# Moving the own-edge additions of the second graph convolution into the middle of the layer norm, on one Trainium2 core

## The chip, the core and the metric

The kernel runs on one core of a Trainium2 chip. Five engines work side by side and meet only at semaphores: TensorE (PE, with its weight loads PEld), VectorE (DVE), ScalarE (ACT), GpSimd (POOL) and SyncE (SP), which issues the DMA transfers here. The metric is the device time of one execution in microseconds. Before the change it is 3359.72 us, the median of three runs (3355.37 to 3362.7).

## The reference

Four graph layers are applied one after the other to `x`, 3125 nodes of 128 features, over 53125 edges with self loops, each as `x = x + layer(relu(layernorm(x)))`. The change touches the first half of the second layer, a graph convolution followed by a layer norm and a SiLU:

```python
def _gcn_conv(x, src, dst, W, b, num_nodes):
    h = x @ W
    deg = jnp.zeros((num_nodes,), h.dtype).at[dst].add(1.0)
    dinv = jnp.where(deg > 0, jax.lax.rsqrt(jnp.maximum(deg, 1.0)), 0.0)
    norm = dinv[src] * dinv[dst]
    msg = h[src] * norm[:, None]
    out = jnp.zeros((num_nodes, h.shape[1]), h.dtype).at[dst].add(msg)
    return out + b
...
h = _gcn_conv(h, src, dst, gcn_w, gcn_b, num_nodes)
h = _silu(_layernorm(h, ln_gamma, ln_beta))
h = _gat_conv(h, src, dst, gat_w, att_src, att_dst, gat_b, num_nodes, HEADS)
```

The sum over edges is computed as a product with the adjacency matrix (counts of edges, in float16), to which each node's edge to itself is added.

## The kernel before, in words

`gcn_second` (from L1148) does the second convolution. The 3125 target nodes are cut into eight chunks of 1, 3, 3, 3, 3, 4, 4 and 4 tiles of 128 nodes (`GCN_TILES`), here chunk 0 to chunk 7. For one chunk the five engines do this:

- SP (L1172) loads the chunk's columns of the adjacency matrix into one of two buffers of `cols` (`gcn_adj` in the trace). Chunk c + 2 goes into the buffer of chunk c and is issued when all five casts of chunk c are done.
- DVE adds the own edges (`add_own`, L1223): one small addition of an identity per tile into `cols`. It waits for the load. Its last addition raises `own_in`.
- POOL casts the chunk to fp32r for the matmul (`widen`, L1210), in five groups of five source tiles each, into a ring of four slots `stream` (`gcn_stream`). The first cast of a chunk waits for `own_in`; cast n waits until PE has streamed group n - 4.
- PE does two matmuls for each of 25 source tiles t (L1306). Between them it turns the sums of the chunk before to node order (`turn`, L1281, at t = 5) and, at t = 22, turns that chunk's finished values back to feature order (`turn_back`, L1290), for which it waits for the SiLU of that chunk.
- ACT copies the sums out of PSUM (L1197), takes the square root (L1180), the SiLU (L1182) and the copy of the result (L1188).
- DVE does `norm(c)`: scale and bias from PSUM (L1232), `bn_stats` (L1237), `bn_aggr` (L1241), the addition of epsilon (L1244), then it waits for the square root (`rooted`), reciprocal (L1246), shift (L1248), one scaling per tile (L1251), times gamma (L1254), plus beta (L1256). Each step waits for the one before by the semaphore `steps`.

So norm(c) runs while PE streams chunk c + 1, and its end is what `turn_back` in that same stream waits for. The order on every engine is written out by hand; there is no scheduler. The loop that sets DVE's order is L1268 to L1271.

Of the kernel before, what the change touches and what calls it, by code (L numbers as in the profile page):

```python
# [77 lines left out]
NGC = 8  # L78
# [119 lines left out]
def over_nodes(ap, nt=NT):  # L198

    return ap.unsqueeze(1).to_broadcast([ap.shape[0], nt, ap.shape[1]])  # L200
# [261 lines left out]
class Kernel:  # L462
# [687 lines left out]
    def gcn_second(self, own, parts, out, ht, rows, weights, cols, stream, loaded):  # L1150
# [15 lines left out]
        with nc.Block() as block:  # L1166
            @block.sync
            def _(e):
                for c, (lo, hi) in enumerate(spans):
                    if c >= 2:  # L1170
                        e.wait_ge(widened, NGG * (c - 1))
                        e.dma_start(cols[:, c % 2, 0:(hi - lo) // W, :], self.adj[:, lo // W:hi // W, :]).then_inc(loaded[c % 2], 16)  # L1172
# [43 lines left out]
            @block.vector  # L1216
            def _(e):
                def add_own(c):

                    e.wait_ge(loaded[c % 2], 16 * (c // 2) + 16)  # L1220
                    for i, (t, p) in enumerate(tiles[c]):
                        at = cols[:, c % 2, 8 * i:8 * i + p // W, t * W:(t + 1) * W]
                        inst = e.tensor_tensor(at, at, ident_h[:, 0:p].rearrange("p (w n) -> p w n", n=W), ALU.add)  # L1223
                    inst.then_inc(own_in, 1)

                def norm(c):

                    t0, t1 = tiles[c][0][0], tiles[c][-1][0] + 1
                    at, two = slice(t0, t1), range(t0, t1)
                    e.wait_ge(turned, c + 1)  # L1230
                    for q, (t, p) in enumerate(tiles[c]):
                        inst = e.scalar_tensor_tensor(out[0:p, t, :], ps[0:p, 2 + c % 2, q * P:(q + 1) * P], self.dinv[0:p, t:t + 1],  # L1232
                                                      bias[0:p, :], ALU.mult, ALU.add)
                    inst.then_inc(steps, 1)
                    e.wait_ge(steps, per * c + 1)
                    for t in two:
                        inst = e.bn_stats(out=stats[:, t, :], in_=out[:, t, :])  # L1237
                    inst.then_inc(steps, 1)
                    e.wait_ge(steps, per * c + 2)
                    for t in two:  # L1240
                        inst = e.bn_aggr(out=both[:, t, :], in_=stats[:, t, :])  # L1241
                    inst.then_inc(steps, 1)
                    e.wait_ge(steps, per * c + 3)
                    e.tensor_scalar(scale[:, at], both[:, at, 1], EPS, None, ALU.add).then_inc(steps, 1)  # L1244
                    e.wait_ge(rooted, c + 1)
                    e.reciprocal(scale[:, at], scale[:, at]).then_inc(steps, 1)  # L1246
                    e.wait_ge(steps, per * c + 5)
                    e.scalar_tensor_tensor(shift[:, at], both[:, at, 0], -1.0, scale[:, at], ALU.mult, ALU.mult).then_inc(steps, 1)  # L1248
                    e.wait_ge(steps, per * c + 6)
                    for t in two:  # L1250
                        inst = e.tensor_scalar(out[:, t, :], out[:, t, :], scale[:, t:t + 1], shift[:, t:t + 1], ALU.mult, ALU.add)  # L1251
                    inst.then_inc(steps, 1)
                    e.wait_ge(steps, per * c + 7)
                    e.tensor_tensor(out[:, at, :], out[:, at, :], over_nodes(gamma[:], t1 - t0), ALU.mult).then_inc(steps, 1)  # L1254
                    e.wait_ge(steps, per * c + 8)
                    e.tensor_tensor(out[:, at, :], out[:, at, :], over_nodes(beta[:], t1 - t0), ALU.add).then_inc(steps, 1)  # L1256

                e.tensor_copy(ident_h[:], self.ident[:])
                e.memset(out[:, NT - 1, :], 0.0).then_inc(begun, 1)
                e.wait_ge(begun, 1)  # L1260
                add_own(0)
                for n in range(NT // grp):
                    at = slice(n * grp, (n + 1) * grp)
                    e.wait_ge(near, n + 1)
                    e.tensor_tensor(parts[:, at, 1, :], own[:, at, :], parts[:, at, 0, :], ALU.subtract).then_inc(far, 1)
                add_own(1)
                weights(e, begun)
                for c in range(NGC):  # L1268
                    if c + 1 >= 2 and c + 1 < NGC:
                        add_own(c + 1)  # L1270
                    norm(c)  # L1271

            @block.tensor
# [1730 lines left out]
```

## Time and profile before

| | |
|---|---|
| median of three runs | 3359.72 us |
| profiled execution | 3363.56 us, span 3361.9 us |
| busy: PE, DVE, ACT, POOL | 83%, 52%, 41%, 29% of the span |
| second convolution | about 417 to 525 us of the span |
| casts L1210, all 40 | 417.6 to 509.8 us |

The profile is of one execution, with times counted from the span's start. The second convolution is about 3% of the span. A row of a timeline merges neighbouring instructions of one line: start, length of the whole group, engine, line, operation, written and read tensors, and `xN` for the count; what stands in brackets is the idle time before it and what ended it. Idle time of an engine counts only where another engine then waits.

### The profile page before, as it was taken

What the parts mean: (1) busy time and instruction counts of PE and PEld (TensorE: products, weight loads), DVE (VectorE), ACT (ScalarE), POOL (GpSimd) and SP (SyncE); (2) the same over time, 40 slices, a digit from 0 to 9 for tenths busy, and PEclk for the clock granted to TensorE, in tenths of its full rate; (3) what the DMA queues carried; (4) which work ended last, traced back from release to release, by engine and by line L of the source; (5) the groups of instructions that cost most, each with busy time, mean ns of one, the idle gap of its engine ahead of it and who ended that gap; (6) DMA issues with size and microseconds to landing.
All of it is one profiled execution on the core that took longest, in us unless ns stands there. A gap on an engine that the chain in (4) does not pass through costs nothing. (4 is left out here: it accounts for less than half of the span.)

```text
span 3361.9 us, 41194 instructions
## 1 busy us (share of the span) xinstructions
PE 2803.2 (83%) x13998; PEld 2153.0 (64%) x13998; DVE 1752.6 (52%) x4008; ACT 1368.4 (41%) x2596; POOL 965.7 (29%) x786
## 2 busy tenths in 40 slices
PE   6778797999996999999999999999744455447997
PEld 3446684777774778778887877786433344435775
DVE  8997657999977351121111112112544443356994
ACT  4573134999996121111111111111413333342896
POOL 6110070000000643223222322220177777740000
PEclk9998897999998999999999999999855555555999
DMA  4434352111002432212121212210242221113200
GB/s 151 144 105 157 137 200 88 40 40 77 8 1 92 162 117 88 79 59 98 59 94 68 88 64 98 85 64 5 87 129 47 46 55 29 29 19 128 79 35 20
DMA packets 79695, 266.66 MB, mean 79 GB/s; under 512 B 21129, under 2 KB 53344, under 8 KB 70176
## 3 DMA queue, kind: packets, MB, share of 16 engines
q1 hardware_dynamic: 62520, 236.50, 18.9%
q0 software_dynamic: 16976, 27.54, 3.8%
q8 instruction: 121, 1.98, 0.3%
q14 instruction: 78, 0.64, 0.1%
HBM read 232.80 MB, written 31.18 MB: 79 GB/s over the span
## 5 line engine op out<-in xcount | busy, mean ns | idle before, releaser
L2798 PE MATMUL psum<-gate_stream,parts 128*128 128x384 f32 (+1 forms) x3600 | 668.8, 344 | 15.9 <-POOL gate_stream L2871 11.6
L2798 PEld LDWEIGHTS psum<-gate_stream,parts 128*128 128x128 f32 x3600 | 632.4, 189 | 32.9 <-issue 13.4
L2871 POOL CAST gate_stream<-gate_adj 128x1920 fp32r<-128x1920 f16 (+1 forms) x200 | 370.6, 1860 | 851.9 <-PE psum L2798 829.7
L2150 PE MATMUL psum<-gat_h,gat_pair 128*128 128x129 f32 (+1 forms) x3750 | 571.9, 292 | 8.6 <-DVE gat_pair L1954 7.8
L2150 PEld LDWEIGHTS psum<-gat_h,gat_pair 128*128 128x128 f32 (+1 forms) x3750 | 462.4, 191 | 123.3 <-issue 77.9
L1482 POOL DMA_INDIRECT edge_rows<-edge_table,src_idx x440 | 429.8, 977 | 181.4 <-issue 133.8
L2889 DVE SCALAR_TENSOR_TENSOR gate_work<-psum,bhh,gate_work 128x384 f32<-128x384 f32 (+1 forms) x80 | 50.0, 626 | 793.7 <-PE psum L2761 763.1
L1954 DVE SCALAR_TENSOR_TENSOR gat_pair<-gat_above,gat_adj 128x512 f32<-128x512 f32 (+3 forms) x525 | 326.4, 622 | 87.7 <-PE psum L2150 58.7
L2063 ACT ACTIVATE gat_above<-psum,gat_as 128x512 f32<-128x512 f32 (+3 forms) x525 | 329.4, 627 | 42.7 <-PE psum L2138 41.0
L2054 ACT ACTIVATE psum<-gat_ad_rows,gat_as 128x512 f32<-128x512 f32 (+3 forms) x525 | 334.9, 638 | 16.8
L1909 DVE SCALAR_TENSOR_TENSOR gat_acc<-gat_adj,gat_q,gat_acc 128x512 f32<-128x512 f16 (+3 forms) x497 | 328.3, 677 | 0.0
L2815 ACT COPY x<-psum 128x384 f32<-128x384 f32 (+1 forms) x72 | 31.8, 488 | 545.5 <-PE psum L2798 545.5
L1719 PE MATMUL psum<-edge_rows,edge_hot 128*128 128x81 f32 x826 | 179.6, 418 | 85.7 <-DVE edge_rows L1618 85.7
L1719 PEld LDWEIGHTS psum<-edge_rows,edge_hot 128*128 128x128 f32 x826 | 177.2, 332 | 87.4 <-issue 87.0
L966 PE MATMUL psum<-count_hot,count_low 128*128 128x400 f16 x611 | 171.2, 382 | 50.6 <-DVE count_hot L887 34.5
L2138 PE MATMUL psum<-gat_r_rows,gat_pick 6*128 6x512 bf16 (+7 forms) x525 | 189.4, 362 | 0.9 <-ACT gat_r_rows L2072 0.9
L2843 ACT ACTIVATE gate_work<-psum,brz 128x384 f32<-128x384 f32 (+1 forms) x80 | 47.0, 587 | 331.7 <-PE psum L2774 331.7
L966 PEld LDWEIGHTS psum<-count_hot,count_low 128*128 128x128 f16 x611 | 87.4, 144 | 136.2 <-issue 112.7
L887 DVE TENSOR_SCALAR count_hot<-iota_hot,keyt 128x400 f16<-128x400 f16 x611 | 168.6, 336 | 3.0 <-PE psum L966 2.4
L2382 POOL MEMSET parts<- 128x512 f32 x1 | 0.5, 524 | 546.2 <-POOLq L2282 546.2
L981 ACT CAST count_stage<-psum 128x400 f16<-128x400 f32 x196 | 96.7, 493 | 91.6 <-PE psum L966 89.4
L1646 ACT ACTIVATE edge_hot<-iota,edge_minus 128x128 f32<-128x128 f32 x413 | 121.3, 392 | 8.0 <-PEq L2457 8.0
(484 smaller groups left out, 3700.1 us busy)
## 6 DMA issues: line engine op xcount, KB each, us to landing
gate_adj<-adj SPq DMA_DIRECT2D x35, 2400.0 KB, 8.1
gat_adj<-adj SPq DMA_DIRECT2D x8, 3200.0 KB, 10.8
adj<-count_stage SPq DMA_DIRECT2D x196, 100.0 KB, 1.7
gcn_adj<-adj SPq DMA_DIRECT2D x8, 2400.0 KB, 8.1
edge_place<-row_scratch SPq DMA_DIRECT2D x40, 352.0 KB, 3.6
gate_adj<-adj SPq DMA_DIRECT2D x5, 2800.0 KB, 9.0
gcn_adj<-adj SPq DMA_DIRECT2D x4, 3200.0 KB, 10.0
edge_rows<-edge_table,src_idx POOLq DMA_INDIRECT x440
```

Of the source, the lines that this page charges most:

```text
L887: e.tensor_scalar(hot[:, j % HRING, :], iota_hot[:], keyt[:, j:j + 1], None, ALU.is_equal).then_inc(hots, 1)
L966: e.matmul(flat[:, bass.ds(at[j % RL], ROW)], low[:, j // LS % LRING, :, j % LS], hot[:, j % HRING, :], start=False, stop=False, skip_grou ...
L1482: e.indirect_dma_start(out=rows[:, c % 2, s, 0:ROWS], out_offset=None, in_=table, in_offset=bass.IndirectOffsetOnAxis(ap=self.src_idx[:, k ...
L1719: mm = e.matmul(flat[:, bass.ds(to[k % 4], SUMS)], hot_of(c)[:, s, :], rows[:, c % 2, s, :], start=False, stop=False, skip_group_check=True)
L1909: e.scalar_tensor_tensor(on, of, q[:, hi, h:h + 1], on, ALU.min, ALU.max).then_inc(most, 1)
L1954: e.scalar_tensor_tensor(on(pair, g % 2), on(above, g % 3), 1e30, cols[:, u % ring, 0:width(u) // W, hi * W:(hi + 1) * W], ALU.min, ALU.mu ...
L2054: e.activation(ps[:, 4 + g % 3, 0:up - lo], ad_rows[:, h, lo:up], ACT.Relu, bias=as8[:, hi, h:h + 1], scale=1.0 - NEG).then_inc(relus, 1)
L2063: e.activation(above[:, g % 3, 0:width(u)], ps[:, 4 + g % 3, 0:width(u)], ACT.Exp, bias=as2[:, hi, h:h + 1]).then_inc(exps, 1)
L2138: e.matmul(ps[:, 4 + g % 3, 0:width(u)], pick[:, h, :], r2_rows[:, u % 2, 0:width(u)], start=False, stop=False, skip_group_check=True).the ...
L2150: mm = e.matmul(ps[0:p, b, a:a + D + 1], pair[:, g % 2, i * P:i * P + p], h1[:, hi, h, :], start=hi == 0 and i % 3 == 0, stop=hi == NT - 1 ...
L2798: mm = e.matmul(ps[:, f, 0:hi - lo], parts[:, t, m, f, :], stream[:, (NGG * i + t // GG) % GR, 0:windows(i), t % GG * W:(t % GG + 1) * W], ...
L2871: e.tensor_copy(stream[:, n % GR, 0:windows(i), :], cols[:, i % 2, 0:windows(i), g * GW:(g + 1) * GW]).then_inc(widened, 1)
```

## The change

The own edges of chunk c + 2 are no longer added after norm(c) but inside it: behind the addition of epsilon and ahead of the wait for the square root. Chunks 2 to 7 are concerned; chunks 0 and 1 keep their place ahead of the loop. The two new lines shift the later line numbers by two: L1246, L1248, L1251, L1254 and L1256 become L1248, L1250, L1253, L1256 and L1258.

```diff
@@ -1242,6 +1242,8 @@
                     inst.then_inc(steps, 1)
                     e.wait_ge(steps, per * c + 3)
                     e.tensor_scalar(scale[:, at], both[:, at, 1], EPS, None, ALU.add).then_inc(steps, 1)
+                    if c + 2 < NGC:
+                        add_own(c + 2)
                     e.wait_ge(rooted, c + 1)
                     e.reciprocal(scale[:, at], scale[:, at]).then_inc(steps, 1)
                     e.wait_ge(steps, per * c + 5)
@@ -1266,8 +1268,6 @@
                 add_own(1)
                 weights(e, begun)
                 for c in range(NGC):
-                    if c + 1 >= 2 and c + 1 < NGC:
-                        add_own(c + 1)
                     norm(c)
```

DVE's instructions from the epsilon of chunk 1 to the own edges of chunk 3, before (`h_23` is the convolution's output, `gcn_ident` the identity):

```order
L1244 TENSOR_SCALAR gcn_scale<-gcn_both 128x3
L1246 RECIPROCAL gcn_scale<-gcn_scale 128x3
L1248 SCALAR_TENSOR_TENSOR gcn_shift<-gcn_both,gcn_scale 128x3
L1251 TENSOR_SCALAR h_23<-h_23,gcn_scale,gcn_shift 128x128 x3
L1254 TENSOR_TENSOR h_23<-h_23,ln_gamma 128x384
L1256 TENSOR_TENSOR h_23<-h_23,ln_beta 128x384
L1223 TENSOR_TENSOR gcn_adj<-gcn_adj,gcn_ident 128x8x16 x3
```

The same stretch of DVE after the change:

```order
L1244 TENSOR_SCALAR gcn_scale<-gcn_both 128x3
L1223 TENSOR_TENSOR gcn_adj<-gcn_adj,gcn_ident 128x8x16 x3
L1248 RECIPROCAL gcn_scale<-gcn_scale 128x3
L1250 SCALAR_TENSOR_TENSOR gcn_shift<-gcn_both,gcn_scale 128x3
L1253 TENSOR_SCALAR h_23<-h_23,gcn_scale,gcn_shift 128x128 x3
L1256 TENSOR_TENSOR h_23<-h_23,ln_gamma 128x384
L1258 TENSOR_TENSOR h_23<-h_23,ln_beta 128x384
```

The three additions of L1223 have moved past six lines of the norm. The other engines' instructions stand in the same order as before; on POOL the first cast of chunk 3 still waits for the last of these three additions.

## Rows read from the trace of the kernel before

**Rows 1.** Engine busy times by stretch, the stretches from chunk 1's turn to chunk 7's.
```profile
core 0: us, PE busy (x) PEld busy (x) DVE busy (x) ACT busy (x) POOL busy (x), PEclk, DMA share, GB/s
441.88:515.68 73.80, 65.15 (x331) 55.74 (x329) 42.19 (x128) 25.20 (x37) 53.63 (x27) 1.00 0.41 162
```

**Rows 2.** Waits of 417 to 526 us: us in total, times, longest.
```profile
PE psum L1290 <- ACT h L1182: 12.9, 7, 6.7
PE psum L1306 <- POOL gcn_stream L1210: 1.8, 4, 0.9
```

**Rows 3.** Timeline of DVE, second half of the norm of chunk 2.
```profile
454.62 0.76 DVE L1244 TENSOR_SCALAR gcn_scale<-gcn_both 128x3 f32<-128x3 f32 x1
455.65 0.18 DVE L1246 RECIPROCAL gcn_scale<-gcn_scale 128x3 f32<-128x3 f32 x1 [0.27 <-ACT gcn_scale L1180]
455.86 1.25 DVE L1248 SCALAR_TENSOR_TENSOR gcn_shift<-gcn_both,gcn_scale 128x3 f32<-128x3 f32 x1
457.14 0.86 DVE L1251 TENSOR_SCALAR h<-h,gcn_scale,gcn_shift 128x128 f32<-128x128 f32 x3
...
459.11 0.49 DVE L1223 TENSOR_TENSOR gcn_adj<-gcn_adj,gcn_ident 128x128 f16<-128x128 f16 x3
```

**Rows 4.** Timeline of POOL: the casts of chunks 3, 4, 6 and 7.
```profile
448.36 8.73 POOL L1210 CAST gcn_stream<-gcn_adj 128x1920 fp32r<-128x1920 f16 x5 [3.21 <-DVE gcn_adj L1223]
459.66 8.74 POOL L1210 CAST gcn_stream<-gcn_adj 128x1920 fp32r<-128x1920 f16 x5 [2.56 <-DVE gcn_adj L1223]
...
485.19 11.41 POOL L1210 CAST gcn_stream<-gcn_adj 128x2560 fp32r<-128x2560 f16 x5 [2.70 <-DVE gcn_adj L1223]
499.79 10.08 POOL L1210 CAST gcn_stream<-gcn_adj 128x2240 fp32r<-128x2240 f16 x5 [3.19 <-DVE gcn_adj L1223]
```

**Rows 5.** Timeline of PE: the turns back of chunk 0 and chunk 2.
```profile
438.95 0.27 PE L1290 MATMUL psum<-ident,h 128*128 128x128 f32 x1
...
459.80 0.55 PE L1290 MATMUL psum<-ident,h 128*128 128x128 f32 x3 [1.21 <-ACT h L1182]
```

**Rows 6.** Timeline of ACT, chunk 0.
```profile
435.98 0.31 ACT L1182 ACTIVATE h<-h 128x128 f32<-128x128 f32 x1 [0.16 <-DVE h L1256]
```

**Rows 7.** Groups by form: count | busy us, mean ns of one | idle before.
```profile
L1248 DVE SCALAR_TENSOR_TENSOR gcn_shift<-gcn_both,gcn_scale 128x3 f32<-128x3 f32 x4 | 4.4, 1105 | 0.1
L1244 DVE TENSOR_SCALAR gcn_scale<-gcn_both 128x3 f32<-128x3 f32 x4 | 4.1, 1023 | 0.1
L1248 DVE SCALAR_TENSOR_TENSOR gcn_shift<-gcn_both,gcn_scale 128x4 f32<-128x4 f32 x3 | 3.4, 1144 | 0.1
L1244 DVE TENSOR_SCALAR gcn_scale<-gcn_both 128x4 f32<-128x4 f32 x3 | 2.0, 661 | 0.1
```

**Rows 8.** The gated layer, DVE additions beside POOL casts: timelines, and L2904's durations (min/median/max).
```profile
1130.01 9.92 POOL L2871 CAST gate_stream<-gate_adj 128x1920 fp32r<-128x1920 f16 x5 [7.63 <-PE psum L2798]
...
1132.35 4.20 DVE L2904 TENSOR_TENSOR state<-gate_work 128x384 f32<-128x384 f32 x2
...
L2904 DVE TENSOR_TENSOR state<-gate_work x80: 548/550/2414, 1132.4 to 2344.5; 128x384 f32<-128x384 f32 x70, 128x448 f32<-128x448 f32 x10
```

**Rows 9.** A tensor_scalar with a column scalar: durations min/median/max.
```profile
L887 DVE TENSOR_SCALAR count_hot<-iota_hot,keyt x611: 302/314/8215, 35.9 to 292.2; 128x400 f16<-128x400 f16 x153
```

**Rows 10.** Two stretches after a pause of PE, columns as in rows 1.
```profile
1218.00:1221.40 3.40, 3.40 (x14) 3.12 (x13) 1.32 (x2) 0.68 (x2) 0.92 (x1) 0.50 0.00 0
...
2344.40:2351.20 6.80, 5.74 (x7) 2.52 (x8) 1.74 (x6) 0.24 (x1) 0.70 (x3) 0.50 0.17 52
```

**Rows 11.** Timeline of PE around those pauses.
```profile
1216.65 0.63 PE L2734 MATMUL psum<-ident,state 128*128 128x128 f32 x4 [2.88 <-DVE parts L2912]
1217.04 1.06 PE L2798 MATMUL psum<-gate_stream,parts 128*128 128x448 f32 x4
1218.58 1.84 PE L2798 MATMUL psum<-gate_stream,parts 128*128 128x448 f32 x4
...
2345.46 3.75 PE L2491 MATMUL psum<-state,l 128*128 128x512 f32 x4 [4.34 <-PEq L2710]
```

## Prediction

> **What bounds the kernel now.** I read the busy times by stretch first. From the turn of chunk 1 to that of chunk 7, 73.80 us, TensorE is busy for 65.15 us [rows 1]; DVE and POOL have slack. So at most 8.65 us is to be had from PE's gaps here, 0.26% of the whole. The waits then say who holds PE: the SiLU ahead of the turn back, 7 times, 12.9 us, of which 6.7 us is the last one, behind the stream; and the POOL casts, 4 times, 1.8 us [rows 2]. The SiLU waits for DVE's norm. Thus in each chunk from 1 on the norm's length sits on PE's path: turn, norm, SiLU, turn back, 6 + 10 matmuls, next turn.
>
> The timelines of DVE and POOL are to be laid over each other [rows 3, 4]. In the norm of chunk 2 the epsilon addition, three numbers per partition, takes 0.76 us, the shift 1.25 us; the reciprocal between them, of the same size, 0.18 us. The five casts of chunk 3 run from 448.36 to 457.09, one per 1.75 us, so one ends near 455.35 and the last at 457.09. The epsilon ends at 455.38 and the shift at 457.11: each waited for the end of a cast. From 457.14 on POOL is idle, and the rest of the norm (L1251, L1254, L1256) runs free. It is idle because the own edges of chunk 4 come only at 459.11 + 0.49; the next cast starts at 459.66 [rows 3, 4]. POOL's 2.56 us of idle time is what shields the tail of the norm.
>
> That such waits come for every such instruction is seen in the gated layer: two additions of 128x384 with both inputs in SBUF take 4.20 us together beside casts, 2.1 us each, where the median of the line is 0.55 us; and five casts take 9.92 us instead of 8.73 [rows 8, 4]. DVE and POOL take turns, one instruction each, though DVE's next is ready.
>
> The Trainium skill states this as a rule (SBUF — State Buffer, Who interferes with whom): DVE and GpSimd share a port pair under an exclusive lock held for the whole instruction; a DVE instruction with two SBUF inputs contends with a GpSimd one that reads SBUF, and tensor_scalar can too. By that rule, with which these rows agree, the change is a harmful one.
>
> **The change part by part.** Nothing is added or removed in count; 21 additions of own edges, of chunks 2 to 7, move from behind the norm into its middle.
>
> *Own edges.* Three cost 0.49 us, four about 0.62 (0.14 us more for each). 0.27 us of it lies under the wait for the square root [rows 3]: +0.22 or +0.35 us, for norms 0 to 5 three times each, +1.7 us. The reciprocal then lies under the first cast, 0.2 us six times, -1.2. Net +0.5 us.
>
> *Casts in the tail.* When the own edges of chunk c + 2 are in, its first cast starts. Its ring slot is free: it needs the second group of chunk c + 1, which PE finished before norm(c) began its epsilon. The second and third cast need the third and fourth group, which PE streams at 1.8 us each before it stops at t = 22; the fourth cast needs the last group, which lies behind the turn back. So exactly three casts fall into the tail. The tail's instructions that want the shared port are the shift, L1251 once per tile, L1254, L1256: more than three, each followed by a gap for a dependence or a dispatch. By the alternation seen in [rows 8], the three casts stand in the norm in full: shift behind the first, the first L1251 behind the second, the others behind the third. Prices, by start to start in [rows 4]: 1.75 us for 128x1920, 2.28 for 128x2560 (11.41 / 5), 2.02 for chunk 7. Chunks 2 to 4: 9 x 1.75 = 15.7; chunks 5 and 6: 6 x 2.28 = 13.7; chunk 7: 3 x 2.02 = 6.1. Together +35.5 us.
>
> The doubtful part is whether L1251 wants the port. An epsilon addition is a tensor_scalar and does [rows 3]; one with a column scalar, L887, does 400 elements in 0.314 us [rows 9], more than one element per ns, so the form has the fast mode as well. I take it that it does. If not, the L1251s run under the second cast: 0.86 us in norms 1 to 4, about 1.1 in norm 5, 0.35 in norm 0, so 4.9 us less.
>
> The skill's page names tensor_scalar from SBUF to SBUF as able to use both ports; by it the sum keeps these 4.9 us, and no row here shows a two-column form beside a cast.
>
> *Norm 0 has slack.* Its SiLU ends at 435.98 + 0.31 while PE comes to the turn back at 438.95, unheld [rows 5, 6]: 2.6 us of its three casts are hidden. Its own edges meet a last cast of chunk 1, +0.3. Together -2.3 us.
>
> *What goes.* The last cast of chunk c + 1 starts about when turn(c) does and ends before the epsilon, since POOL is now ahead. A free instruction of this size takes near the 0.18 us of the reciprocal [rows 3], say 0.17. Epsilon: 4.1 + 2.0 us for seven, less 7 x 0.17, 4.9 us. Shift: 4.4 + 3.4 less 7 x 0.16 is 6.7 us [rows 7]; the first cast's wait is already among the three. PE's waits for casts: 1.8 us [rows 2]. Together -13.4 us. Norm 6 has no own edges and gains only; PE can use all but 0.3 us of it, +0.3.
>
> Sum so far: 0.5 + 35.5 - 2.3 - 13.4 + 0.3 = +20.6 us.
>
> *TensorE's clock.* PE waits 1.2 us for the SiLU today [rows 5] and would wait some 4.5 to 6 us in chunks 2 to 6, near 3 in chunk 1. The granted clock is 1.00 in this stage [rows 1]. After pauses of 2.88 and 4.34 us it was 0.50, that is 1.2 instead of 2.4 GHz, for stretches of 3.40 and 6.80 us, with PE busy for 3.40 and 5.74 us of them [rows 10, 11]. Four matmuls then took 1.84 us and not 1.06 [rows 11], so 43% of the busy time is lost. Lower end 0 (no fall). Upper end: all 16 matmuls between turn back and turn at half clock, 2.9 us of them becoming 5.1, 6 x 2.2 = 13. I take the shorter of the two stretches, 0.43 x 3.4 = 1.46 us, six times: +8.8 us.
>
> Total +29.4 us: 3363.56 + 29.4 = 3393.0 in a profiled execution. That one ran 3.8 us above the median of the runs, so for the median 3359.7 + 29.4 = 3389.1 us, 0.9% slower.
>
> **Rivals.** A measurement of this kernel tells some 0.2%, 6.7 us, from no change.
>
> *A, part of the price.* L1251 doesn't want the port (15.7 us), or the clock holds (20.6), or it holds and L1251 is out too: 3375 to 3384 us. For it: the two-column form takes 0.29 us a tile, no quicker than an addition would; against: rows 9, and no pause above 2.8 us in these rows without a fall.
>
> *B, one cast only.* If DVE's queued instructions went ahead of the next cast, only the first would be paid: 35.5 becomes 11.8, sum -3.1 without stalls for the clock, 3357 us. Against it stand the two additions of 4.20 us.
>
> *C, faster.* The tail is shielded after all, if the ring slot for the first cast of chunk c + 2 became free only after the norm: POOL's 13.4 us of waits in norm and stream would go and nothing come. PE can give at most its 8.65 us of gaps, less own edges: about -7, 3353 us. It decides at the second group of chunk c + 1: streamed after the norm's end, C; before the epsilon, my case. That group is done some 2 us after turn(c), the epsilon 2.5 us after it.
>
> *D, the load is late.* Own edges now wait 3.7 us earlier for the load of chunk c + 2, with DVE's tail behind them. The load is issued at the last cast of chunk c, which also moves ahead, by 3 us or more. If it were late by 2 us in five norms: +10 more, 3399 us.
>
> **How the numbers follow.** My case (all three casts, L1251 among the held, clock falling) 0.55; A 0.27; D 0.06; B 0.08; C 0.04. The forecast is my case's 3389 us. Low: A's lower half reaches 3375, and B and C lie outside; with part of a cast less than I count, 3368. High: the clock's upper end adds 4, a little of D the rest: 3400. Slower by over 0.2%: my case, A and D, 0.88; within 0.2%: B, 0.08; faster: C, 0.04.
>
> **What would show it.** Right: the casts of chunk c + 2 start right behind L1223 in the middle of norm(c), three in a row, a pause, then two; epsilon near 0.17 us, shift near 1.6 (2.1 beside 128x2560), L1251 three in over 2 us, one of L1254 or L1256 free; norms of 10 to 12 us instead of 5.5 to 8.5; PE waiting some 25 us in total for the SiLU within the stream, none for casts; a clock of 0.50 in stretches between 440 and 540 us. L1251 unmoved at 0.86 us and L1254 and L1256 both long: A. Tail as before: B or C. Waits of L1223 for a load: D. All outside this stage should stay.

## Result: 0.65% slower, and the profile after

| | median | runs | profiled execution | from the first turn to the eighth |
|---|---|---|---|---|
| before | 3359.93 us | 6 | 3363.56 us | 432.83 to 515.68, 82.85 us |
| after | 3380.12 us | 6 | 3375.06 us | 432.74 to 539.41, 106.67 us |

The ratio is 1.0065, 95% interval 1.0054 to 1.0075; on 3359.7 us that is 18 to 25 us. The forecast was 3389 us, range 3368 to 3400. The measure for the stage in all that follows is the time from the start of the turn of chunk 0 to the start of that of chunk 7 (L1281 on PE); it grew by 23.8 us. The two profiled executions differ by 11.5 us only, because the one after was the fastest of its six, and lies 5 us below their median, and the one before 4 us above its own. The stage is where the change is to be read, the medians say what it costs.

The timeline of DVE after the change, in the norms of chunk 0 and chunk 2 (start, length, engine, line, operation, count):

```profile
435.07 0.15 DVE L1248 RECIPROCAL gcn_scale<-gcn_scale 128x1 f32<-128x1 f32 x1
435.25 1.76 DVE L1250 SCALAR_TENSOR_TENSOR gcn_shift<-gcn_both,gcn_scale 128x1 f32<-128x1 f32 x1
437.04 1.77 DVE L1253 TENSOR_SCALAR h<-h,gcn_scale,gcn_shift 128x128 f32<-128x128 f32 x1
438.85 1.76 DVE L1256 TENSOR_TENSOR h<-h,ln_gamma 128x128 f32<-128x128 f32 x1
440.64 0.29 DVE L1258 TENSOR_TENSOR h<-h,ln_beta 128x128 f32<-128x128 f32 x1
...
460.98 0.87 DVE L1232 SCALAR_TENSOR_TENSOR h<-psum,dinv,gcn_bias 128x128 f32<-128x128 f32 x3 [6.77 <-PE psum L1281]
...
462.94 0.17 DVE L1244 TENSOR_SCALAR gcn_scale<-gcn_both 128x3 f32<-128x3 f32 x1
463.02 0.49 DVE L1223 TENSOR_TENSOR gcn_adj<-gcn_adj,gcn_ident 128x128 f16<-128x128 f16 x3
...
463.63 1.74 DVE L1250 SCALAR_TENSOR_TENSOR gcn_shift<-gcn_both,gcn_scale 128x3 f32<-128x3 f32 x1
465.41 3.75 DVE L1253 TENSOR_SCALAR h<-h,gcn_scale,gcn_shift 128x128 f32<-128x128 f32 x3
469.20 0.56 DVE L1256 TENSOR_TENSOR h<-h,ln_gamma 128x384 f32<-128x384 f32 x1
469.79 0.56 DVE L1258 TENSOR_TENSOR h<-h,ln_beta 128x384 f32<-128x384 f32 x1
```

The same stretch of POOL, the casts of chunk 2 and of chunk 4:

```profile
435.21 5.26 POOL L1210 CAST gcn_stream<-gcn_adj 128x1920 fp32r<-128x1920 f16 x3 [0.41 <-DVE gcn_adj L1223]
442.78 3.54 POOL L1210 CAST gcn_stream<-gcn_adj 128x1920 fp32r<-128x1920 f16 x2 [2.31 <-PE psum L1306]
...
463.58 5.25 POOL L1210 CAST gcn_stream<-gcn_adj 128x1920 fp32r<-128x1920 f16 x3 [1.10 <-DVE gcn_adj L1223]
473.85 3.65 POOL L1210 CAST gcn_stream<-gcn_adj 128x1920 fp32r<-128x1920 f16 x2 [5.02 <-PE psum L1306]
```

In norm 2 the epsilon is free now (0.17 us against 0.76 in [rows 3]) and the own edges follow it. Then three casts run from 463.58 to 468.83; DVE's shift, first and second scaling each stand behind one of them, and the rest of the norm's tail (times gamma and plus beta, L1256 and L1258) is free from 469.20 on. The norm, L1232 to L1258, takes 9.37 us (460.98 to 470.35) and not 6.54. Norm 0 shows the turn-taking at its plainest: three different instructions of 0.15 to 0.35 us in rows of 1.76, 1.77, 1.76, one per 1.80 us. Three casts, a pause until PE has turned back, two casts: as the ring of four slots allows.

The waits of the stretch 417 to 546 us (total, times, longest), the answer to [rows 2]:

```profile
POOL gcn_stream L1210 <- PE psum L1306: 32.8, 10, 6.5
...
PE psum L1290 <- ACT h L1182: 24.1, 6, 5.8
```

PE waits 24.1 us for the SiLU inside the stream, where it waited 6.2; it waits for no cast any more. And the clock, busy times by stretch with the columns of [rows 1], and PE's timeline at the turns back of chunks 0 and 1:

```profile
432.74:539.41 106.67, 81.94 (x384) 73.27 (x382) 64.01 (x140) 28.79 (x42) 61.48 (x31) 0.87 0.34 135
441.33:444.31 2.98, 2.98 (x18) 2.94 (x19) 0.00 (x0) 1.81 (x3) 1.53 (x1) 1.00 0.23 97
453.40:460.20 6.80, 5.38 (x18) 5.38 (x19) 0.77 (x2) 2.76 (x4) 1.79 (x1) 0.50 0.01 2
```

```profile
441.33 0.33 PE L1290 MATMUL psum<-ident,h 128*128 128x128 f32 x1 [2.28 <-ACT h L1182]
441.41 3.06 PE L1306 MATMUL psum<-gcn_stream,gcn_parts 128*128 128x384 f32 x16
...
454.82 0.90 PE L1290 MATMUL psum<-ident,h 128*128 128x128 f32 x3 [4.06 <-ACT h L1182]
455.37 5.24 PE L1306 MATMUL psum<-gcn_stream,gcn_parts 128*128 128x384 f32 x16
```

After a wait of 2.28 us the clock stays at 1.00 and 16 matmuls take 3.06 us; after one of 4.06 us it is 0.50 (1.2 GHz) from 453.4 to 460.2 and they take 5.24.

### The profile page after: what moved, and what is told of

The parts are those of the page before. It is cut to its first block and busy times, and to the rows that moved or that the text cites. A ratio compares the mean times of both kernels' runs of the same rounds, so it can differ in the third digit from the quotient of the medians.

```text
span 3373.4 us, 41194 instructions
## 1 busy us (share of the span) xinstructions
PE 2794.7 (83%) x13998; PEld 2147.6 (64%) x13998; DVE 1771.9 (53%) x4008; ACT 1368.4 (41%) x2596; POOL 965.2 (29%) x786
## 3 DMA queue, kind: packets, MB, share of 16 engines
q8 instruction: 121, 1.98, 0.2%
## 5 line engine op out<-in xcount | busy, mean ns | idle before, releaser
L2798 PE MATMUL psum<-gate_stream,parts 128*128 128x384 f32 (+1 forms) x3600 | 667.1, 344 | 15.9 <-POOL gate_stream L2871 11.5
L2798 PEld LDWEIGHTS psum<-gate_stream,parts 128*128 128x128 f32 x3600 | 630.8, 188 | 32.7 <-issue 13.4
L1482 POOL DMA_INDIRECT edge_rows<-edge_table,src_idx x440 | 429.3, 976 | 178.9 <-issue 133.8
L1210 POOL CAST gcn_stream<-gcn_adj 128x1920 fp32r<-128x1920 f16 (+3 forms) x40 | 74.5, 1890 | 182.8 <-DVE gcn_adj L1223 150.0
```

The lines of the kernel that those rows point to most:

```text
L1482: e.indirect_dma_start(out=rows[:, c % 2, s, 0:ROWS], out_offset=None, in_=table, in_offset=bass.IndirectOffsetOnAxis(ap=self.src_idx[:, k ...
L2798: mm = e.matmul(ps[:, f, 0:hi - lo], parts[:, t, m, f, :], stream[:, (NGG * i + t // GG) % GR, 0:windows(i), t % GG * W:(t % GG + 1) * W], ...
```

## The experiments

Each edit is to the kernel after, if nothing else is said. "Stage" is the time between the same two turns, from the profile of that kernel; the "tail" of a norm is its part behind the own edges, from the shift on. Ratios are to the kernel before, run beside it on the same chip.

| | stage, us | median, us | ratio (95%) |
|---|---|---|---|
| before | 82.85 | | 1 |
| after | 106.67 | 3380.12 | 1.0065 (1.0054 to 1.0075) |
| after again (e8) | 106.89 | 3380.25 | 1.0066 (1.0053 to 1.0080) |
| casts held until the norm is over (e1) | 84.44 | 3362.78 | 1.0010 (1.0001 to 1.0019) |
| one cast let into the norm (e2) | 83.53 | 3360.29 | 1.0003 (0.9994 to 1.0012) |
| PE kept busy in its pauses (e3) | 99.39 | 3379.12 | 1.0056 (1.0043 to 1.0068) |
| the same, longer in chunk 4 (e7) | 97.87 | 3374.21 | 1.0045 (1.0031 to 1.0058) |
| scalings on ACT (e5) | 103.31 | 3722.04 | 1.0057 (1.0043 to 1.0070) |
| after again, other chip (e6) | 109.49 | 3728.78 | 1.0063 (1.0042 to 1.0084) |
| kernel before, one cast in five on ACT (e4) | 75.72 | 3352.90 | 0.9982 (0.9973 to 0.9992) |

**e1, the casts held, the own edges still in the middle.**

```diff
                     if g == 0:
                         e.wait_ge(own_in, c + 1)
+                        if c >= 2:
+                            e.wait_ge(steps, per * (c - 1))
```

> The changed kernel, but POOL's first cast of chunk c + 2 also waits until the norm of chunk c is over; the own edges stay in the middle of the norm. Theory (casts stand between the instructions of the norm's tail at the shared port, and PE's longer pauses bring its clock down): norms of 5.7 to 8.7 us as before plus 0.2 to 0.35 us, turn 0 to turn 7 near 83 us instead of 106.7, clock 1.00 throughout, 3357 to 3362 us. Rival (the moved additions themselves, or the load that they now wait for earlier, lengthen the norm): norms stay at 9 to 11 us and the time near 3380 us.

Measured: ratio 1.0010, stage 84.44 us, 1.6 above before and 22.2 below after. What costs is what the move lets start, and not the move itself. The rival is out. Three expectations missed: the norms of chunks 2 to 5 grew by 0.6 to 0.8 us and not by 0.2 to 0.35; the clock was 0.98 in the mean of the stage, with one short fall; and the median of 3362.78 us is just above 3362. The norm of chunk 2 shows why the norms grew by more:

```profile
455.94 0.76 DVE L1246 TENSOR_SCALAR gcn_scale<-gcn_both 128x3 f32<-128x3 f32 x1
456.60 2.15 DVE L1225 TENSOR_TENSOR gcn_adj<-gcn_adj,gcn_ident 128x128 f16<-128x128 f16 x3
458.68 0.16 DVE L1250 RECIPROCAL gcn_scale<-gcn_scale 128x3 f32<-128x3 f32 x1
```

With the casts back at their old time, the last one of chunk 3 falls between the own edges: 2.15 us instead of 0.49, of which the shift's old wait is gone (0.16 instead of 1.25 us in [rows 3]). The fall of the clock comes behind the turn back of chunk 5:

```profile
502.65 1.10 PE L1292 MATMUL psum<-ident,h 128*128 128x128 f32 x4 [1.98 <-ACT h L1182]
```

The 1.6 us of the stage are a sum of three terms, read from the times of turns and turns back in the two profiles. The stretches from a turn to its turn back, in which the norms lie, are 1.9 us longer in all; those from the turns back of chunks 1 to 4 to the next turn are 1.7 us shorter; and the one behind the turn back of chunk 5, with the low clock, is 1.3 us longer (5.51 instead of 4.19 us).

**e2, one cast inside.**

```diff
                     if g == 0:
                         e.wait_ge(own_in, c + 1)
+                    if g == 1 and c >= 2:
+                        e.wait_ge(steps, per * (c - 1))
```

> The changed kernel, but only the first cast of chunk c + 2 may start inside the norm of chunk c; the second waits for the norm's end. Theory (each cast in the tail is paid once, less the fixed part of the instruction that it holds): shift 1.75 to 2.3 us as in the changed kernel, the scalings free at 0.86 us, norms of 6.4 to 8.2 us, no wait for the epsilon, 3357 to 3363 us. Rival (POOL's early start as such, by any number of casts, costs the whole 20 us): 3375 us or more.

Measured: 1.0003, no change, and the stage 0.7 us above before. In the norm of chunk 3:

```profile
467.28 0.77 DVE L1246 TENSOR_SCALAR gcn_scale<-gcn_both 128x3 f32<-128x3 f32 x1
467.95 0.62 DVE L1225 TENSOR_TENSOR gcn_adj<-gcn_adj,gcn_ident 128x128 f16<-128x128 f16 x4
468.49 0.17 DVE L1250 RECIPROCAL gcn_scale<-gcn_scale 128x3 f32<-128x3 f32 x1
468.69 2.28 DVE L1252 SCALAR_TENSOR_TENSOR gcn_shift<-gcn_both,gcn_scale 128x3 f32<-128x3 f32 x1
471.01 0.86 DVE L1255 TENSOR_SCALAR h<-h,gcn_scale,gcn_shift 128x128 f32<-128x128 f32 x3
```

One cast in, one instruction held: the shift 2.28 us beside a cast of 128x2560, the scalings 0.86 us again. "No wait for the epsilon" was wrong: four casts still come after the norm and reach into the next one. One cast in each tail costs the stage next to nothing, three cost it 24 us: the price goes with the number of casts in the tail, not with POOL's early start.

**e5, which instruction is held does not matter.** The scaling per tile (L1253) is taken from DVE; ACT does it as an activation with scale and bias.

```diff
+                    e.wait_ge(steps, per * c + 6)
+                    for t in range(t0, t1):
+                        inst = e.activation(out[:, t, :], out[:, t, :], ACT.Identity, scale=scale[:, t:t + 1], bias=shift[:, t:t + 1])
+                    inst.then_inc(steps, 1)
...
-                    for t in two:
-                        inst = e.tensor_scalar(out[:, t, :], out[:, t, :], scale[:, t:t + 1], shift[:, t:t + 1], ALU.mult, ALU.add)
-                    inst.then_inc(steps, 1)
```

> The changed kernel, with the scalings (L1253, one per tile) done by ACT, so that only the shift and the two long additions of the tail want the port. Theory (DVE and POOL take turns whatever the instructions are, and three casts are ready in each tail): still three casts in the tail, one ahead of the shift, one ahead of the product with gamma, one ahead of the addition of beta; norms of 8.6 to 9.0 us for 3 tiles beside casts of 128x1920, 0.4 to 0.8 us less than in the changed kernel, since the scaling runs under the second cast; 3374 to 3378 us. Rival (the two-column scaling is what the casts collide with): norms of 6.5 to 7 us and 3362 us or less.

Measured on another chip, on which the whole kernel takes 3703 us before and 3729 after; the durations on DVE and POOL are the same there, so the ratio and the stage are read, not the microseconds expected. The norms of 3 tiles beside casts of 128x1920 took 8.59 us (466.71 to 475.30 for chunk 1), as expected, and three casts stood in each tail. DVE's and POOL's timelines in the norm of chunk 1:

```profile
469.37 1.75 DVE L1254 SCALAR_TENSOR_TENSOR gcn_shift<-gcn_both,gcn_scale 128x3 f32<-128x3 f32 x1
472.52 0.73 DVE L1257 TENSOR_TENSOR h<-h,ln_gamma 128x384 f32<-128x384 f32 x1 [1.41 <-ACT h L1183]
473.28 2.02 DVE L1259 TENSOR_TENSOR h<-h,ln_beta 128x384 f32<-128x384 f32 x1
```

```profile
469.31 5.59 POOL L1214 CAST gcn_stream<-gcn_adj 128x1920 fp32r<-128x1920 f16 x3 [1.10 <-DVE gcn_adj L1227]
```

The third cast now stands ahead of the addition of beta, which takes 2.02 us instead of 0.56; the second runs mostly beside ACT's scalings and holds the product with gamma for the rest, 0.73 us. The rival is out: the scaling was only what happened to be next. Beside the changed kernel on the same chip (e6) the stage is 6.2 us shorter, of which 4.3 us lie between turn and turn back; the ratios, 1.0057 and 1.0063, do not tell the two apart.

**e3 and e7, the clock.** Ahead of the wait for the SiLU PE does small matmuls of constants into an unused bank; e7 has 48 of them in chunk 4.

```diff
                         if c and t == 22:
+                            if c < NGC - 1:
+                                self.keep_busy(e, ps[:, 6, :], 20 if c == 1 else 34)
                             turn_back(c - 1)
```

> The changed kernel, with 34 small matmuls (20 in chunk 1) of constants into an unused PSUM bank ahead of each wait for the SiLU in chunks 1 to 6, some 3.6 us of work for PE in its pause. Theory (part of the loss is the clock that falls after the pauses): clock 1.00 from 433 to 540 us, 16 matmuls of 128x384 between turn back and turn in 3.1 us instead of 4.1 to 5.2, 6 to 9 us faster than the changed kernel, 3371 to 3374 us, norms unchanged. Rival (the clock costs nothing, since what it slows is hidden): 3378 to 3382 us.

Measured: the stage 7.3 us shorter, with one fall of the clock left, behind the longest pause (chunk 4). The total, 1.0056, was above the expected 3371 to 3374 us, and its interval overlaps that of the kernel after; it could not tell the theory from the rival. So a version with the longest pause closed as well (e7) and the changed kernel (e8) were run side by side.

> e3_busy with 48 instead of 34 small matmuls in chunk 4, whose pause is the longest (5.8 us), beside the unchanged changed kernel on the same chip. Theory (the clock costs some 7 us of the changed kernel): clock 1.00 in the whole stage, turn 0 to turn 7 near 98 us, and a time 5 to 10 us below that of e8_again, the ratio to the kernel before near 1.004. Rival (what the clock gives in the stage is lost elsewhere, as the totals of e3_busy left open): the same ratio as e8_again within 2 us.

> The changed kernel, the partner of e7_busy2. Theory: ratio to the kernel before 1.006 to 1.007, turn 0 to turn 7 of 105 to 110 us, depending on where the clock falls after each pause. Rival: a ratio near 1.004 or below would say that the first comparison was high by chance.

Measured: 3374.21 against 3380.25 us, 6.0 us, and in the stage 97.87 against 106.89 us, 9.0 us. The intervals of the two ratios overlap a little, but each of the five runs of e7 (3369.82 to 3376.93 us) lies below each of the five of e8 (3378.38 to 3382.47). In e7 the whole stretch, and the 16 matmuls after the turn back of chunk 2, read:

```profile
432.50:531.00 98.50, 96.22 (x591) 85.27 (x591) 63.97 (x140) 29.13 (x42) 61.44 (x31) 1.00 0.37 146
```

```profile
468.62 0.55 PE L1290 MATMUL psum<-ident,h 128*128 128x128 f32 x3 [0.33 <-ACT h L1182]
468.92 3.05 PE L1308 MATMUL psum<-gcn_stream,gcn_parts 128*128 128x384 f32 x16
```

The clock is 1.00 throughout. DVE's 63.97 us busy are those of the kernel after, 64.01: nothing changed in the norms. So 9.0 us of the stage's 24 are the clock. The other 15 remain at full clock: what the casts cost at the port, less what became free. Whether all of the 9.0 reach the total stays open; 6.0 were seen, and in the profiles 1.6 us of the 9.0 are lost again just behind the stage (54.4 us from the last turn to the first of the matmuls with `gat_pair` in e7, 52.9 in e8).

**e6, the changed kernel a second time.**

> The changed kernel once more, for a second profile. Theory: turn 0 to turn 7 again within 2 us of 106.7 us, whatever the whole takes, and 3375 to 3385 us; differences of more than 3 us between two profiles lie outside the second convolution. Rival (the whole and the stage vary together): the stage differs by as much as the whole does.

Measured: 1.0063 on the chip of 3703 us. The stage was 109.49 us, 2.8 above the first, where 2 were expected. All eight norms had the lengths of the first profile within 0.06 us. Of the 2.8 us, 2.5 lie between turns back and turns, where PE waits for nothing and its clock sets the time. One difference is that the clock also fell behind the turn back of chunk 0, after a wait as short as 2.32 us, and it took 4.2 us from there to the next turn instead of 3.0:

```profile
461.02 0.33 PE L1290 MATMUL psum<-ident,h 128*128 128x128 f32 x1 [2.32 <-ACT h L1182]
462.00:465.50 3.50, 3.50 (x15) 3.41 (x14) 0.00 (x0) 1.76 (x2) 1.82 (x2) 0.57 0.00 0
```

So what varies in the stage is the clock; and e8, on a chip like the first, gave 106.89.

**e4, a version that beats both.** If casts, tail and own edges queue at one port, the remedy is less work there. In the kernel before, ACT does the first cast of chunks 2 to 7 behind the SiLU, with a semaphore of its own (`acted`) for PE and for the load; POOL does the other four.

```diff
                     e.activation(out[:, t0:t1, :], out[:, t0:t1, :], ACT.Silu).then_inc(eased, 1)
+                    if c + 2 < NGC:
+                        n, k = NGG * (c + 2), (spans[c + 2][1] - spans[c + 2][0]) // W
+                        e.wait_ge(own_in, c + 3)
+                        e.wait_ge(streamed, n - GS + 1)
+                        e.copy(stream[:, n % GS, 0:k, :], cols[:, c % 2, 0:k, 0:GW]).then_inc(acted, 1)
...
-                    for g in range(NGG):
+                    for g in range(1 if c >= 2 else 0, NGG):
                         widen(c, g)
```

> The kernel before, with the first of the five casts of chunks 2 to 7 done by ACT behind the SiLU, four left to POOL. Theory (the five casts, the norm's tail and the own edges follow one another at the shared port and make the period of a chunk of 11.3 us, above PE's 10.3): casts end 1.75 to 2.3 us earlier, epsilon and shift wait less, PE's waits for the SiLU nearly go, 4 to 8 us faster than before, 3352 to 3356 us. Rival (ACT's cast delays its copy of the sums and the square root, and PE waits there): 3359 us or slower.

Measured: 0.9982 (0.9973 to 0.9992), stage 75.72 us, 7.1 less than before. Beside it, DVE in the norm of chunk 2 and POOL's and ACT's casts:

```profile
455.00 0.78 DVE L1253 TENSOR_SCALAR gcn_scale<-gcn_both 128x3 f32<-128x3 f32 x1
...
456.25 0.17 DVE L1257 SCALAR_TENSOR_TENSOR gcn_shift<-gcn_both,gcn_scale 128x3 f32<-128x3 f32 x1
```

```profile
458.97 7.00 POOL L1219 CAST gcn_stream<-gcn_adj 128x1920 fp32r<-128x1920 f16 x4 [3.22 <-DVE gcn_adj L1232]
```

```profile
458.96 1.79 ACT L1191 CAST gcn_stream<-gcn_adj 128x1920 fp32r<-128x1920 f16 x1
```

The shift no longer waits, and a norm takes 5.47 us (453.03 to 458.50) instead of 6.54. ACT's cast takes 1.79 us while POOL's beside it keep their 1.75 each, so the two do not hold each other up. PE's wait for the SiLU within the stream is down to 0.3 us in total, and from the turn of chunk 2 to that of chunk 3 it is 10.23 us (452.50 to 462.73) instead of 11.32 (452.12 to 463.44). So the chain of five casts, the shift held by the last of them, the tail and the own edges set the chunk's period before as well. How much of the 7.1 us is the port and how much POOL's shorter queue was not told apart.

## Why the prediction was right, point by point

- *Where the time goes* was right in its main steps: own edges early, first cast right behind, three casts in the tail, a pause, two more; epsilon free; L1253 among the held; norm 0 partly covered; no wait for a load. e1, e2 and e5 show it from three sides. Of the signs that I named, two missed: the norms took 9.4 us (chunks 1 and 2) to 11.3, not 10 to 12, and both L1256 and L1258 were free, not one of them.
- *The price of the casts* was the mis-sized term. I counted each cast with its full 1.75, 2.28 or 2.02 us and then the held instruction's own time as well. Most of that time runs under the cast. Norm 0 shows it: slots of 1.79 to 1.81 us that hold an instruction which free takes 0.16, 0.35 and 0.29 us; so a cast adds 1.60, 1.42 and 1.47 us. In norms 1 and 2 the shift adds 1.75 - 0.16 and the scalings 3.75 - 0.86 us, together 4.5 where I had 5.2; in norms 3 and 4 it is (2.28 - 0.16) + (4.82 - 0.86) = 6.1 against 6.8; norm 5 (2.02 - 0.16) + (4.54 - 1.12) = 5.3 against 6.1. Over six norms 4.5 + 9.0 + 12.2 + 5.3 = 31 us and not 35.5. With it the sum without the clock is 16.1 us; the stage of e7, whose clock does not fall, is 15.0 above before. The profiles show where the last 1 us is. The stretches from turn to turn back are 17.9 us longer in e7 than before (74.19 against 56.26), which is the mended sum without PE's waits for casts. The stretches from turn back to turn are 2.9 us shorter (23.68 against 26.59), where I had put 1.8 for those waits. Why it is more was not followed.
- *The clock* was put at 8.8 us by six stalls of 1.46; measured 9.0 in the stage, by five. From the turn back to the next turn the kernel after takes 5.63, 4.52, 5.22, 5.39 and 6.32 us and e7 3.21, 3.19, 3.78, 4.12 and 3.95: a fall cost 1.3 to 2.4 us, 1.8 in the mean, and not most behind the longest wait. The wait of 2.28 us in chunk 1 brought no fall, those of 3.8 to 5.8 us all did. That 8.8 came so near to 9.0 is luck: six falls too cheap against five dearer ones.
- *What goes* (13.4 us) was right in kind: epsilon and shift of norm 6 free, no wait of PE for a cast; in size it was 1.1 us short, as said.
- *The forecast's 29.4 us* thus becomes 24 in the stage and 20 to 23 in the medians. The rest, 1 to 4 us, stays open. In the profiles of the kernel after and of e8 the first matmul of the gated layer still comes 24 and 25 us later than before (1123.0 and 1124.3 against 1099.1 us). Behind the whole stage, the shortest times are those same two (2834 and 2837 us; in the other profiles, without those of the chip of 3703 us, it is 2841 to 2849). One profile of the kernel before is too few to say whether the last layers give something back or only scatter.
- *Rival A* (part of the price) came nearest in its time: the measured 3380 lies in its 3375 to 3384, and 9 us below my case. But it was for other reasons than it gave: L1253 did want the port and the clock did fall. B, C and D did not occur.

The Trainium skill's rule on the port (SBUF — State Buffer, Who interferes with whom) agrees with all of these rows, also for a tensor_scalar with two column scalars, for which no row before had spoken: 1.77 us beside a cast, 0.35 alone.

## What to carry to other kernels

An idle engine is not always free: POOL's wait for its input was what kept it out of VectorE's way on the critical path. Before an instruction is moved forward, look at what its semaphore releases, and which VectorE instructions (here those with two inputs in SBUF, and tensor_scalar from SBUF to SBUF) then run beside GpSimd casts; each can cost one GpSimd instruction, less nearly the whole of its own time. Where both queue for the port, ScalarE can take some of the work (e4). A stall of TensorE of 4 to 6 us cost a further 1.3 to 2.4 us here for its clock.

## What the runs showed of the hardware that was not expected

- The time that a held VectorE instruction adds is the GpSimd instruction less nearly the whole of its own length: 1.79 to 1.81 us per turn with an instruction of 0.16, 0.35 or 0.29 us in it.
- The length of one pause of PE does not settle whether the clock falls. Waits of 2.28 us (after) and 2.17 (e8) ahead of the turn back of chunk 0, and of 1.97 (e1) ahead of that of chunk 3, were followed by a clock of 1.00. Lower clocks followed one of 2.32 (e6, chunk 0: 0.57 in the row shown), one of 2.43 (e2, chunk 3: 0.66 from 473.67 to 478.67), one of 1.98 (e1, chunk 5: 0.59 from 502.0 to 506.0) and one of 2.88 us in the gated layer (0.50, [rows 10, 11]).
- The kernel before took 3703 us on one chip and 3358 on another. For the changed kernel, 3729 and 3380 us, the profiles show where most of it is: POOL's indirect DMA issues of the edge gathers (L1482) waited 490 us in e6, of which 312 for PE, and 179, none of them for PE, in the kernel after. The norms of the stage looked at here had the same lengths on both. Why that chip is slower was not followed.
